# Two edits in the graph stage of a fused graph, LSTM and layer-norm kernel: the order of VectorE's Z biases, and the means added quad by quad

## The reference, cut to what matters

```
h = relu(layernorm(x))                                  # statistics over features
h = relu(adj @ (h @ Wg0 + bg0));  h = relu(adj @ (h @ Wg1 + bg1))
for p in 1..4:                                          # windows of p tokens
    last = LSTM_p(windows of h);  h[token p*w + p-1] = last
x = x + h
h = relu(layernorm(x))
x = x + diag(adj)*(h @ W[0]) + triu(adj,1) @ (h @ W[1]) + tril(adj,-1) @ (h @ W[2]) + bias
```

## Time and profile before

| | |
|---|---|
| median of 3 runs | 401.04 us (400.91 to 401.04) |
| the profiled execution | 400.5 us |
| its span, first to last instruction | 398.5 us |
| busy share of the span: TensorE, VectorE, ScalarE, GpSimd | 98%, 84%, 71%, 15% |
| granted TensorE clock | 1.0 of full speed throughout |

### The profile page before, as it was taken

One profiled execution on the slowest core, in us unless ns is written; L12 is line 12 of the kernel. 1 busy time (PEld: TensorE's weight loads), 2 busy tenths in 40 slices (PEclk: granted clock), 3 DMA queues, 4 the chain that ended last, 5 costly groups with the idle time before them and its releaser, 6 DMA issues.

```text
span 398.5 us, 6492 instructions
## 1 busy us (share of the span) xinstructions
PE 390.0 (98%) x2346; PEld 340.1 (85%) x2346; DVE 336.1 (84%) x868; ACT 281.0 (71%) x555; POOL 58.9 (15%) x59
## 2 busy tenths in 40 slices
PE   8999999999999999999999999999999999999997
PEld 7787889998876889899777879899887788989886
DVE  6569999998889688797998778989798958787897
ACT  5668777875697686777389677767569868667554
POOL 4910200101240003001140000300123000000250
PEclk9999999999999999999999999999999999999999
DMA  6850000005362000112347000030537200000003
GB/s 208 310 249 2 0 0 2 2 0 107 53 131 57 0 28 0 55 79 57 52 80 159 26 2 27 2 133 0 108 55 134 78 0 28 0 28 1 2 1 132
DMA packets 11263, 23.78 MB, mean 60 GB/s; under 512 B 4576, under 2 KB 5984, under 8 KB 9952
## 3 DMA queue, kind: packets, MB, share of 16 engines
q0 software_dynamic: 2160, 9.44, 12.6%
q1 hardware_dynamic: 9072, 13.94, 10.1%
HBM read 16.01 MB, written 4.22 MB: 51 GB/s over the span
## 4 chain that ended last, share of the span: by engine, by line
PE 57%; DVE 27%; ACT 12%; issue 2%; DMA 1%; POOL 0%; SPq 0%; DVEq 0%; ACTq 0%
PE PS L594 8%; PE PS L603 8%; PE PS L595 8%; ACT GT L913 6%; PE PS L626 4%; PE PS L622 4%; PE PS L623 4%; PE PS L544 4%; PE PS L664 3%; PE PS L656 3%; ACT TC L928 3%; DVE CS L1056 3%; DVE IC L1038 3%; PE PS L534 2%; PE PS L657 2%; PE PS L658 2%
## 5 line engine op out<-in xcount | busy, mean ns | idle before, releaser
L913 ACT ACTIVATE GT<-PS,BG 128x256 f32<-128x256 f32 (+2 forms) x312 | 158.2, 563 | 16.6 <-PE PS L626 14.2
L594 PE MATMUL PS<-HH,WIH 128*128 128x256 f32 (+2 forms) x312 | 106.2, 341 | 0.0
L595 PE MATMUL PS<-HH,WIL 128*128 128x256 f32 (+2 forms) x312 | 102.6, 330 | 0.0
L603 PE MATMUL PS<-HL,WIH 128*128 128x256 f32 (+2 forms) x294 | 97.3, 331 | 0.6
L928 ACT ACTIVATE TC<-CS 128x512 f32<-128x512 f32 (+2 forms) x88 | 44.9, 511 | 45.0 <-DVE CS L1056 33.3
L594 PEld LDWEIGHTS PS<-HH,WIH 128*128 128x128 f32 x312 | 58.8, 188 | 9.6 <-DVE HH L1097 4.2
L428 POOL TENSOR_TENSOR RS<-VE,NHALF 128x4 f32<-128x4 f32 (+2 forms) x18 | 32.9, 1825 | 213.9 <-DVE VE L992 142.5
L595 PEld LDWEIGHTS PS<-HH,WIL 128*128 128x128 f32 x312 | 58.8, 188 | 4.0 <-issue 1.2
L603 PEld LDWEIGHTS PS<-HL,WIH 128*128 128x128 f32 x294 | 55.5, 189 | 6.5 <-DVE HL L1105 2.5
L626 PE MATMUL PS<-SL,WHH 128*128 128x256 f32 (+2 forms) x192 | 60.2, 313 | 0.2
L622 PE MATMUL PS<-SH,WHH 128*128 128x256 f32 (+2 forms) x192 | 60.0, 312 | 0.0
(11 more groups left out here) (99 smaller groups left out, 640.2 us busy)
## 6 DMA issues: line engine op xcount, KB each, us to landing
out_tbd<-X SPq DMA_DIRECT2D x15, 256.0 KB, 2.0
X<-x_tbd SPq DMA_DIRECT2D x3, 1024.0 KB, 13.3
H<-x_dbt SPq DMA_DIRECT2D x3, 1024.0 KB, 5.5
H<-HF POOLq DMA_DIRECT2D x6, 512.0 KB, 4.7
H<-means POOLq DMA_DIRECT2D x6, 512.0 KB, 5.1
X<-bias_row POOLq DMA_DIRECT2D x3, 1024.0 KB, 8.3
WI<-wih_t SPq DMA_DIRECT2D x1, 1024.0 KB, 5.1
X<-x_tbd SPq DMA_DIRECT2D x3, 256.0 KB, 3.4
```

The costliest lines, as they stand in the source:

```text
L594: pe.matmul(dst, WIH[:, p - 1, cols], x_high, start=True, stop=False)
L595: pe.matmul(dst, WIL[:, p - 1, cols], x_high, start=False, stop=False)
L603: mm = pe.matmul(dst, WIH[:, p - 1, cols], x_low, start=False, stop=(j == 0))
L913: act.activation(GT[:, s, q, 0:n], bank(s, q)[:, 0:n], ACT.Tanh if q == C else ACT.Sigmoid, bias=BG[:, 4 * (p - 1) + q:4 * (p - 1) + q + 1 ...
```

## The change

Two edits. On VectorE the two Z biases of stream 1 stand after the second of the last four bn_stats of stream 0, ahead of the other two and of the combination, instead of after the combination. On GpSimd each stream's accumulating transfer of the means is two, one for each quad, with a semaphore for each quad; ScalarE's `turn_up` waits for that of its own quad. This holds for all three graph stages. Nothing else differs.

```diff
-        xt_centred = [sem(f"xt_centred{s}") for s in range(STREAMS)]
+        xt_centred = [sem(f"xt_centred{q}") for q in range(QUADS)]
...
-                    pool.dma_start(turned_stream(s), MEANS[i, s, :].rearrange("(a n) -> a n", a=1).broadcast_to(
-                        [128, HB * T]), accum_op=ALU.add).then_inc(xt_centred[s], 16)
+                    for h in range(HBANKS):
+                        part = slice(h * PACK * T, (h + 1) * PACK * T)
+                        pool.dma_start(turned_stream(s)[:, part], MEANS[i, s, part].rearrange("(a n) -> a n", a=1).broadcast_to(
+                            [128, PACK * T]), accum_op=ALU.add).then_inc(xt_centred[HBANKS * s + h], 16)
...
-                    act.wait_ge(xt_centred[q // HBANKS], 16 * (g + 1))
+                    act.wait_ge(xt_centred[q], 16 * (g + 1))
...
-                stats2(0, i, PACK, HB)
+                stats2(0, i, PACK, PACK + HALF)
+                bias_z(1, i + 1)
+                stats2(0, i, PACK + HALF, HB)
                 combine2(0, i)
-                bias_z(1, i + 1)
                 bias_y(0, i + 1)
```

## The result

The changed kernel takes 402.31 us, median of 11 runs from 400.65 to 404.23; before takes 400.68 us in 11 runs beside it (400.45 to 401.23). The ratio is 1.0044, with a 95% interval of 1.0023 to 1.0065: slower by 0.44%. The prediction said 398.5, between 398.0 and 399.9. The spread is a result too: 0.8 us before, 3.6 us after.

A forecast was written before the change was run, and what follows sets the result against it. TensorE, busy 98% of the span, was taken as the bound. Stage gains of 0.86, 0.88 and 0.81 us sum to 2.55, with no cost elsewhere: 401.04 - 2.55 = 398.5 us, range 398.0 to 399.9.

The forecast's parts named there:

- TensorE's gain: Graph stages: Y of stream 1 follows stream 0's without a hole, saving 0.86, 0.88 and 0.81 us, 2.55 in all.
- Rival A: Graph stages: VectorE, not TensorE, sets the pace and gains 0.49 us each, giving 399.6 us; chance 0.16.
- the cap by VectorE: Next LSTM's first gates: VectorE's low parts limit the gain to 0.88 us a stage, cutting stage 2 from 1.00.
- The write of the means: SP's queue to DRAM: stream 0's means go 1.2 us later, stream 1's 0.49 us sooner.
- and its means with it: Stream 1's means, behind its combination on VectorE, would also come 0.49 us sooner.
- The quads: GpSimd's split transfers: the first of a pair lands in 3.5 us against 5.1 for a whole stream.
- The forecast that no `turn_up` waits: ScalarE: quad 0's means land ahead of need, 0.9 us ahead in stage 3, so nothing waits.
- the sentence on the bias transfer: GpSimd's queue: issue moves by 2 x 0.57 less 0.49 us; at 8.3 us to landing it costs nothing.
- Rival C: LSTM: a wait the traces don't single out takes the gain back, leaving at most 0.8 us, about 400.6; chance 0.08.
- The prediction's own sign of being wrong: Wrong if TensorE's hole is as it was, or the distance between stages doesn't shrink by 0.8 to 0.9 us.
- Rival D: Quad 0's transfer slowed by shared transfer engines, so `turn_up` waits; at 8.3 us landing 10 us, 408.5; chance 0.04.

The follow-up runs named there:

- e3: Changed kernel with the bias row added only to the first of a group's 16 batches (64 KB for 1024 KB); 398.50 us, ratio 0.9945.
- e4: Changed kernel with the bias row's transfer ahead of stream 1's means in GpSimd's queue; 398.45 us, ratio 0.9943.
- g1: Changed kernel with only stream 0's means split into quads and the bias transfer ahead of stream 1's means; 398.51 us, ratio 0.9950.
- g2: Changed kernel with the means of quad 1 added to its first 64 of 512 columns only; 400.21 us, ratio 0.9988.
- g3: Changed kernel with stream 1's means added to the first 64 columns of each quad only; 398.97 us, ratio 0.9963.
- f3: Changed kernel with only stream 0's means split into quads, stream 1's one transfer; 399.76 us, ratio 0.9984.
- f2: Changed kernel with the bias transfer ahead of stream 1's means and each stream's means in one transfer; 402.58 us, ratio 1.0044.
- e1: Kernel before with only the new order of the Z biases, each stream's means one transfer; 401.44 us, ratio 1.0028.
- f4: Kernel before with two more powers, results unused, in GpSimd's queue ahead of each bias row's transfer; 404.85 us, ratio 1.0101.

## Why the prediction was wrong

**TensorE's gain** was right in its mechanism and nearly in its size. 2.55 us were forecast, 0.86, 0.88 and 0.81 by stage; 0.83, 0.67 and 0.80 came. With the bias transfer out of the way (e3, e4, g1) the time is 398.45 to 398.51 us against 398.5 forecast, though from a before of 400.5 to 400.6 and not 401.04. The gain there is 2.0 to 2.2 us, and the match to the tenth is luck: two errors of 0.4 us cancel. Rival A did not hold, but the cap by VectorE bit more than worked out in stage 2. VectorE had 0.46 us of idle time there ahead of its first statistics, from an X that it had just written itself. Counted from the first Z matmul its low parts (L1024) came 0.35 us sooner and not 0.49, and V to the first gate took 3.71 us instead of 3.50.

**The write of the means** was placed right for stream 0: GpSimd issued its quads at 104.26, 198.28 and 296.16, counted from the first Z matmul 1.0, 0.9 and 1.0 us later than before; 1.2 was forecast. For stream 1 the sentence "and its means with it" held for the issue of the write, 0.3 to 0.5 us sooner, and not for its landing, 1.5, 0.7 and 0.7 us later. The first stream's means went 1.2 to 1.35 us later, so the second write runs beside the first stream's accumulating transfers for 3.7 to 5.1 us of its time, where it did for 1.4 to 2.3. It took 5.1 to 5.5 us and not 3.1 to 4.4 (g2 bears this out in stages 1 and 2). The Trainium skill has a rule that would explain it, in DMA: Bandwidth & Descriptors, section "Queues, rings and completion order": each DMA engine alternates between the queues that have work, a packet at a time. These runs show the slower landing, not the alternation.

**The quads** were mis-sized. I took 3.5 us to landing. The first of a pair landed in 4.6, 4.8 and 4.8 us, the second in 5.4 to 6.6. So half the size saves 0.3 to 0.5 us and not 1.6. The difference by the rate of the Trainium skill, which I set aside, was an estimate of 0.6 (DMA: Bandwidth & Descriptors, section "Anatomy of one DMA"). It was nearer, though its 2.6 us for a quad, an estimate too, was further off. The forecast that no `turn_up` waits held, but in stage 3 only just: the quad landed at 300.92 and `turn_up` began at 300.94, where 0.9 us to spare were forecast.

**The failed step is the sentence on the bias transfer**: "at 8.3 us it costs nothing". It took the transfer's landing time as fixed, and it has no row of its reader and none of its slack, which was 2.5 to 2.8 us. For the issue it counted 2 x 0.57 less 0.49 = 0.65 us later; counted from the first Z matmul the issue came 1.95, 0.84 and 0.80 us later, so this was nearly right in stages 2 and 3, and too small in stage 1, where the write of stream 1's means was 1.5 us late. The reader moved up by the gain as well. By the forecast's own figures some 1.0 us of the 2.5 would have been left (2.5 - 0.65 - 0.88). What broke it in stage 2 is the landing time, which grew from 8.0 to 11.8 us. Of these 3.8 us, 0.76 are the longer issue (0.90 to 1.66 us). From the first gate to the landing it is 5.3 us more in stage 2, against 2.5 of slack. By the medians the largest part comes with the quads of stream 1 right ahead of it in the same queue (g3: 3.3 us; f3: 2.5), the next with the data of stream 0's second quad (g2: 2.1). They overlap, since a wait only begins where the slack ends.

Two more sentences of the prediction fell with it. Rival C, a wait in the LSTM that takes the gain back, was the one that came true, and the time went past its 400.6; against it stood that "no transfer on that path has a date of its own", and the bias transfer has one. The prediction's own sign of being wrong showed too: from the first gate of one stage to that of the next the distance shrank by 0.41 us from stage 1 to 2 (94.44 to 94.03) and grew by 2.16 from 2 to 3 (94.76 to 96.92).

**Rival D** was slower too, with another reader: quad 0's `turn_up` never waited in the changed kernel. It had transfers that share queue and engines, as the runs do, but the wrong reader. Its chance of 0.04 was too low, since the case "a transfer further back in that queue" was not among the rivals at all.

**The split** is not a mistake by itself. The new order needs it for quad 0 (f2 without it is 4.1 us slower than e4 with it). It is not needed in stream 1, where it only lengthened the queue.

What stays open: why e1's bias transfer took 9.7 and 10.7 us behind whole transfers, how much of its lateness is due to SP's store beside it, and why two quads take longer than one transfer of the same bytes. The packet counts (432 for two quads and the bias row, 288 for one whole transfer and the bias row) go with that, but no run sets them apart from the rest. How the lower clock adds to a slow execution was seen in a profile of f4 alone.

## What to carry to other kernels

When an edit makes compute earlier or puts a transfer more into a queue, follow the queue to its end: for each transfer behind the edit, find its reader and the slack to it, in each stage, before it is called free. A transfer's landing time is not a constant of its size: here it went with what was ahead of it in its queue and under way beside it. Where one transfer in a queue has its inputs early and its reader early, issue it early: here that turned a loss of 0.44% into a gain of 0.57%, though only together with the split of stream 0's means (f2).

## What the runs showed of the hardware

- 1024 KB accumulated from DRAM into SBUF took 8.0 to 12.9 us from issue to landing, with the same bytes and the same form, depending on what was ahead of it and beside it. 256 KB took 4.4 to 4.8 us as the first of a pair in the profile of the changed kernel, and 4.4 to 6.8 us counted over both of a pair.
- A write of 1024 means, 4 KB, took 2.8 us at its fastest (g2, stream 0) and up to 7.7 us (e4) beside accumulating transfers.
- Each transfer of GpSimd's queue was 144 packets by the page's count, at 256, 512 and 1024 KB alike.
- GpSimd's issue of the bias transfer took 0.9 us where the power beside it ended within 0.05 us of the issue's start, and 1.0 to 2.1 us where the two overlapped for longer. In before and f4 the landing, counted from the start of the issue, was 8.0 to 8.3 us with the short issue and 8.3 to 9.3 with the long one.
- After a hole of 1.81 us TensorE's granted clock fell to its lower level for 3.4 us in one execution (f4); after the hole of 2.40 us in the profile of the changed kernel the clock stayed at 1.0.
